# Graph network kernel: the third graph's input loaded and split earlier, the second adjacency loaded in two halves

## What is computed

```python
A = (adj != 0).astype(x.dtype)
h = x
for l in range(5):
    m = jnp.einsum('bnd,de->bne', h, weight[l])
    agg = jnp.einsum('bij,bid->bjd', A, m)
    gi = agg @ w_ih.T + b_ih
    gh = h @ w_hh.T + b_hh
    r = sigmoid(gi_r + gh_r)
    z = sigmoid(gi_z + gh_z)
    n = tanh(gi_n + r * gh_n)
    h = (1.0 - z) * n + z * h
x = layernorm(x + h * mask)
```

## Time and profile before

| | us |
|---|---|
| median of 3 runs (493.0 to 493.22) | 493.06 |
| the profiled execution | 493.06 |
| its span, first to last instruction | 491.3 |

### The profile page before, as it was taken

How to read it: one execution, slowest core, us unless ns; L and a number is a source line. 1 busy time by engine, 2 the same in 40 slices (tenths; PEclk the granted TensorE clock), 3 DMA queues, 4 the chain that set the end, 5 groups by cost and what they waited for, 6 DMA issues and landing times.

```text
span 491.3 us, 7178 instructions
## 1 busy us (share of the span) xinstructions
PE 480.5 (98%) x2301; PEld 229.6 (47%) x2301; DVE 352.4 (72%) x659; ACT 303.6 (62%) x537; POOL 334.5 (68%) x378
## 2 busy tenths in 40 slices
PE   7999999999999999999999999999999999999994
PEld 5444444444444444444444444444444444564554
DVE  3777867696867687778587777877668675445796
ACT  4556655655655656776657775576765776655564
POOL 3654774748775698997689748659996776334466
PEclk9999999999999999999999999999999999999998
DMA  8878252565535537264955476323443233322313
GB/s 271 258 172 157 45 150 54 151 155 140 120 63 151 118 88 184 57 142 107 175 112 163 106 211 166 73 43 77 89 106 83 57 65 63 65 43 42 83 45 86
DMA packets 133676, 55.72 MB, mean 113 GB/s; under 512 B 97297, under 2 KB 125414, under 8 KB 133638
## 3 DMA queue, kind: packets, MB, share of 16 engines
q1 hardware_dynamic: 108356, 32.39, 32.1%
q10 hardware_dynamic: 25282, 22.87, 14.9%
HBM read 27.46 MB, written 4.19 MB: 64 GB/s over the span
## 4 chain that ended last, share of the span: by engine, by line
PE 83%; POOL 6%; DVE 3%; DMA 3%; ACT 2%; issue 2%; POOLq 0%; DVEq 0%; ACTq 0%
PE pA L790 24%; PE pR L795 6%; PE pR L797 6%; PE pR L796 6%; PE pZ L797 6%; PE pZ L796 6%; PE pZ L795 6%; PE pIN L795 3%; PE pHN L795 3%; PE pHN L796 3%; PE pHN L797 3%; PE pIN L797 3%; PE pIN L796 3%; POOL ZH L528 2%; POOL HT L539 1%
## 5 line engine op out<-in xcount | busy, mean ns | idle before, releaser
L539 POOL TENSOR_TENSOR HT<-H,HT 128x512 f16<-128x512 f32 x76 | 91.8, 1208 | 90.1 <-ACT HT L1167 90.1
L790 PE MATMUL pA<-A,NAT 128*128 128x512 fp8e4 x640 | 151.0, 379 | 0.0
L528 POOL TENSOR_TENSOR ZH<-Z,H 128x512 f32<-128x512 f32 (+1 forms) x80 | 102.6, 1283 | 28.7 <-ACT Z L1182 27.2
L1422 DVE SCALAR_TENSOR_TENSOR T<-pHN,BHN,R 128x512 f32<-128x512 f32 (+1 forms) x80 | 59.9, 749 | 78.2 <-ACT R L1174 77.8
L1187 ACT ACTIVATE pIN<-T,COLS 128x512 f32<-128x512 f32 (+1 forms) x80 | 55.2, 691 | 71.1 <-DVE T L1426 71.0
L790 PEld LDWEIGHTS pA<-A,NAT 128*128 128x128 f16 x640 | 62.5, 98 | 74.8 <-issue 1.0
L1167 ACT ACTIVATE HT<-H 128x512 f16<-128x512 f32 x76 | 47.8, 628 | 64.8 <-DVE H L1436 64.6
L1432 DVE SCALAR_TENSOR_TENSOR pIN<-Z,pIN 128x512 f32<-128x512 f32 (+1 forms) x80 | 55.1, 689 | 24.4 <-ACT pIN L1187 24.2
L1174 ACT ACTIVATE R<-pR,BRZ 128x512 f32<-128x512 f32 (+1 forms) x80 | 54.3, 679 | 20.1 <-PE pR L797 19.4
L1436 DVE TENSOR_TENSOR H<-ZH,pIN 128x512 f32<-128x512 f32 (+1 forms) x80 | 54.8, 685 | 10.1 <-POOL ZH L528 7.7
L1416 DVE TENSOR_TENSOR AG<-pA,AG 128x512 f16<-128x512 f32 x80 | 54.7, 684 | 7.7 <-ACT AG L1163 7.7
(11 more groups left out here) (284 smaller groups left out, 810.1 us busy)
## 6 DMA issues: line engine op xcount, KB each, us to landing
AS<-in_adj_dram ACTq DMA_DIRECT2D x13, 1024.0 KB, 5.9
XR<-in_x_dram ACTq DMA_DIRECT2D x16, 256.0 KB, 2.9
XS<-in_x_dram ACTq DMA_DIRECT2D x13, 256.0 KB, 3.3
out_dram<-Y SPq DMA_DIRECT2D x16, 192.0 KB, 2.2
AS<-in_adj_dram SPq DMA_DIRECT2D x2, 1024.0 KB, 8.7
AS<-in_adj_dram SPq DMA_DIRECT2D x4, 256.0 KB, 5.4
NAT<-HT SPq DMA_TRANSPOSE x64, 3.2
XS<-in_x_dram SPq DMA_DIRECT2D x3, 256.0 KB, 7.8
```

The lines of the kernel that those rows point to most:

```text
L528: g_.tensor_tensor(ZH[:, cs], Z[:, cs], H[:, b, cs], ALU.mult).then_inc(zh_p, 1)
L539: g_.tensor_tensor(HT[:, b, 1, :], H[:, b, :], HT[:, b, 0, :], ALU.subtract).then_inc(h_lo, 1)
L790: last = mm(pA2[:, k % 2, :], NAT[:, k % 2, h, i, :], A8[:, b, i, :], start=(h == 0 and i == 0), stop=(h == 1 and i == NI - 1))
L1422: v.scalar_tensor_tensor(out=T[:, cs], in0=pHN[:, cs], scalar=BHN[:, 0:1], in1=R[:, cs], op0=ALU.add, op1=ALU.mult).then_inc(t_v, 1)
```

## The change

Four places are edited. SyncE issues the load of graph 2's input ahead of the second adjacency (graph 1's), and that adjacency goes out as two transfers of two blocks each, with a semaphore for each half (ld_a1_0 for the first, ld_a[1] for the second, whose later counts stay as they were). VectorE's first cast of graph 1 waits for the first half's semaphore only. ScalarE makes graph 2's high half ahead of the gates of step 0, and GpSimd makes its low half ahead of ZH of step 0.

```diff
+        ld_a1_0 = sem("ld_a1_0")
...
             load_x(1)
-            load_a(1)
             load_x(2)
+            for h in range(2):
+                sp.dma_start(AS[:, 1, 2 * h:2 * h + 2, :],
+                             adj[1, 2 * h * P:2 * h * P + 2 * P, :].rearrange("(i p) n -> p i n", p=P))\
+                    .then_inc([ld_a1_0, ld_a[1]][h], 16)
             load_a(2)
             load_x(3)
...
             natural_lo(1)
+            natural_lo(2)
             kept_share(0)
-            natural_lo(2)
             first_state(1)
...
             transposed_hi(1, pF)
+            natural_hi(2)
             act.wait_ge(cols_v, 1)
             reset_gate(0)
             update_gate(0)
-            natural_hi(2)
             new_gate(0)
...
             def cast_half(b, h):
-                dve.wait_ge(ld_a[b % 3], 16 * (b // 3 + (b % 3 > 0)))
+                if b == 1 and h == 0:
+                    dve.wait_ge(ld_a1_0, 16)
+                else:
+                    dve.wait_ge(ld_a[b % 3], 16 * (b // 3 + (b % 3 > 0)))
```

## The result

| | median us | runs | lowest to highest |
|---|---|---|---|
| before | 493.01 | 9 | 492.66 to 493.98 |
| changed | 494.5 | 9 | 492.93 to 495.73 |

The account below looks back on a forecast made before the run. TensorE, busy 98% of the span, bounds the kernel. Loss of 0.99 us at the casts less 0.47 gained at the transposing transfer gives +0.52: 493.06 to 493.6 us, range 492.5 to 494.7.

Parts of the forecast that it names:

- rival (c): GpSimd's low half goes first at 13.58, ZH before graph 1's second cast: +1.60 us, 494.7; chance 0.15.
- that of being wrong on the high side: Sign in the changed trace: first cast takes 1.7 us and ZH stands between the two casts.
- I take that the first cast wins and runs 13.61 to 14.29: Near tie on VectorE and GpSimd: graph 1's first cast beats the low half asking at 13.58.
- the two steps behind it: Low half ends 1.02 to 1.05 us after first cast, second cast 0.55 after that: 0.99 us loss.
- The gain: Earlier transposing transfer of graph 2 removes TensorE's wait at pHN of step 2: at most 0.47 us.
- The landing of the second half: Second half of graph 1's adjacency lands at 14.5, 0.9 us later than the whole did.
- parts 1 and 2: Reordered loads: x2 at 11.3, first half 12.9; ScalarE's high half 12.87 to 13.50, before the gate: no cost.
- part 4: Low half collides with graph 1's casts at 13.61; the delay reaches AG of step 1 whole: +0.99 us.
- Carried to the end: TensorE has no hole from 24 to 100 us, so any gain or loss before passes through unchanged.
- Rival (a): Casts stay together, GpSimd waits them out, nothing lost: 492.6, or 492.9 in a variant; chance 0.17 with variant.

Follow-up runs that it names:

- the second measurement: The changed kernel run again with no edit: 494.25 us (11 runs), ratio 1.0014 to the kernel before.
- the typical execution: Profiled execution of the unedited changed kernel's repeat, as long as that repeat's median: 494.27 us.
- the loads alone: Against the changed kernel, both halves of graph 2 back in their old places, reordered and halved loads kept: 492.92 us, ratio 0.9994.

## Why the prediction was right in part

**Direction and place: right, shown.** The changed kernel is slower, by the collision of graph 2's low half with the casts of graph 1, and the time of 494.5 lies in the range. Taking only GpSimd's edit back removes the loss. That the time lies in the range is owed to rival (c), for which the range was drawn up to 494.7: the forecast itself, 493.6, had 0.5 of the 1.5 us between the medians (1.1 in the second measurement). Of the signs named beforehand, that of being wrong on the high side came true in the typical execution: a first cast of about 1.7 us, and ZH between the two.

**The step that failed: "I take that the first cast wins and runs 13.61 to 14.29".** In both profiled executions of the changed kernel, and in the one with ZH held back, the low half was recorded 0.05 us ahead of the cast and went first, at its full 1.16 us. The time at which it would ask was right (13.51 against a cast at 13.56, where I had 13.58 against 13.61); who wins was not. I had leaned on one pair, 312.54 against 312.60, over the rule of the Trainium skill, SBUF — State Buffer, section Who interferes with whom (whichever issues first holds the shared ports); taken by the recorded starts, the rule gives the right order at this meeting in every profiled execution in which the two met, with differences from -0.05 us (GpSimd first) to +0.03 and +0.09 (the cast first). But the pair at 312 us was no accident either: it stands in all twelve profiled executions, each time with GpSimd recorded 0.06 us ahead and the cast going first. In the typical execution of the changed kernel:

```profile
313.63 0.37 DVE L1505 BATCH_NORM_AGGREGATE MV<-ST 128x2 f32<-128x6 f32 x4
313.85 1.74 POOL L543 TENSOR_TENSOR HT<-H,HT 128x512 f16<-128x512 f32 x1 [3.39 <-ACT HT L1171]
313.91 0.66 DVE L1417 TENSOR_SCALAR A<-AS 128x1024 fp8e4<-128x1024 f32 x1
```

So the recorded starts of two operations do not tell the order where they lie less than a tenth of a microsecond apart: 0.05 ahead GpSimd went first at 13 us, 0.06 ahead it went second at 312 us. The two meetings differ in GpSimd's operation and in that of VectorE ahead of the cast; whether either decides is not shown. What stood in place of my step is rival (c), with its second meeting: I had it at +1.60 and 494.7, the typical execution ran 2.00 us late at the second cast (2.07 in (c)) and reached pHN 1.36 us late, median 494.25 to 494.5. I gave it 0.15, which was too little with the start times in its favour and a single pair, with another operation of GpSimd, against it.

**The size of the two steps behind it: right.** A cast behind a GpSimd operation ends 0.55 us after it, a low half or a first state of GpSimd behind a cast 1.01 to 1.02, ZH 1.12 to 1.13. Where the order is set as I assumed it, by a tenth of a microsecond, the median is 493.24 against my 493.6: the loss was as put down (second cast to 16.09 against 14.89, in an execution whose casts began 0.23 us later: 0.97), the gain larger, 0.64: 0.33 us net, which is what the trace shows at pHN.

**The gain: right in kind, mis-sized.** I used TensorE's recorded hole of 0.47 us. From the start of the weight transposes to pHN it is 1.07 us before, 0.60 in the run with the low half after the casts, which still waits a little for the transfer, and 0.43 in the typical execution: 0.47 to 0.64. A matmul is recorded for 0.38 us while the next one starts 0.22 after it, so a recorded hole is about 0.16 short of the time lost. This also goes for the three holes of the typical execution: 1.49 us recorded, 2.00 lost.

**The landing of the second half: 14.5 was one end.** In the nine profiles with the halves it landed between 13.54 and 14.15 in five, the typical execution (13.54) and the loads alone (13.64) among them, and between 14.48 and 14.59 in four. With the loads as changed, the first half and the input were in time everywhere, so parts 1 and 2 cost nothing, as put down. The "both holes of the first 24 us" of part 4 are those behind 12 us; TensorE has others before that, which the change does not reach.

**Carried to the end: held.** In the typical execution TensorE is filled from 24 to 100 us (76.00 of 76.00 us), and the time moved by 1.21 us for 1.36 at pHN. Where the missing 0.15 went I did not follow; at 312 us the delay is still 1.31 (313.91 against 312.60).

**Rival (a): answered.** It needed the second cast to follow the first at once with GpSimd waiting. Where both casts were ready and GpSimd waited, in the run with the adjacency in one piece, GpSimd went between them.

**Left open:** what decides when the two are recorded within a tenth of a microsecond, and how often each order comes up, since few executions of each kernel were profiled.

## What to carry to other kernels

An operation moved into an engine's idle gap is free only if the engine that it cannot overlap with is free then too: look at what GpSimd and VectorE's casts do in the same microsecond, and pay the blocked engine's whole delay, not the overlap. When two starts lie within a tenth of a microsecond, the cheap cure is to fix the order with a semaphore wait; here it kept most of the gain (0.47 of 0.64 us) and took the loss away in the profile. A profile of one execution can be the odd one: compare its own time with the median before reading it.

## What the runs showed of the hardware

Four memsets of one column on GpSimd (0.20 us of work), ahead of the operation in dispute, go with a median of 493.24, where the changed kernel has 494.25 and 494.5; in the profiled execution they let the other engine start first.

GpSimd and VectorE's casts took turns at steady prices: a cast (0.68 us alone) held up by GpSimd ended 0.55 us after it, and GpSimd's low half (1.16 us alone) held up by a cast 1.01 to 1.02 after that. At each boundary at the casts of graph 1 the engine that was waiting went next, ahead of the other's next operation, even where that one was ready.

In the execution where the adjacency came in one piece and late, TensorE stood for 2.17 us and then 0.45, and its granted clock fell: 1.00 still in 17 to 18 us, 0.50 in 19 to 21 (the lower of its two levels, 1.2 GHz against 2.4), 0.52 in 21 to 22, then 1.00 again. At the lower level the matmuls of 512 columns started 0.43 us apart instead of 0.22. With holes of 0.6 us or less between 12 and 24 us, as in the typical execution of the changed kernel, it stayed at 1.00.
